# The high part of a normalised row written by ScalarE from x, its f32 row formed a second time by GpSimd

## The reference

```python
x = x + _L0_conv_ref(_gn(x), L0_conv_qkv_w, L0_conv_qkv_b, L0_conv_bias_table)
x = x + _L1_conv_ref(_gn(x), L1_conv_W, L1_conv_b)
...
qkv = (part @ qkv_w.T + qkv_b).reshape(n * NW, WS, 3, N_HEAD, HEAD_DIM)
...
attn = jnp.einsum('wihd,wjhd->whij', q, k)
attn = attn.reshape(n, NW, N_HEAD, WS, WS) + bias[None, None] + MASK[None, :, None]
attn = jax.nn.softmax(attn, axis=-1).reshape(n * NW, N_HEAD, WS, WS)
out = jnp.einsum('whij,wjhd->wihd', attn, v).reshape(n * NW, WS, c)
```

## Time and profile before

| | |
|---|---|
| median of 3 runs | 491.32 us (489.51 to 492.27) |
| the profiled execution | 492.15 us, of which its span is 490.3 us |
| busy share of the span | PE 84%, DVE 82%, ACT 78%, POOL 57% |
| granted TensorE clock, mean | 0.965 |

### The profile page before, as it was taken

The page is one execution under the profiler, slowest core; times in us unless marked ns, Lnnn a source line. Parts: engine busy times, 40 slices in busy tenths (PEclk is TensorE's granted clock), DMA queues, the critical chain, the costliest instruction groups (busy, mean ns, idle before and its releaser), DMA issues.

```text
span 490.3 us, 22208 instructions
## 1 busy us (share of the span) xinstructions
PE 411.5 (84%) x9320; PEld 346.6 (71%) x9320; DVE 400.0 (82%) x872; ACT 381.0 (78%) x913; POOL 280.1 (57%) x392
## 2 busy tenths in 40 slices
PE   0366846989899899988989998899899976799996
PEld 0365735877777778777777877777777765688885
DVE  6766856798789889987988898898787875699887
ACT  3377866898899899898889988899899866646550
POOL 5635746567767766675576677766766547430000
PEclk9987977999999999999999999999999988999999
DMA  6322220233323233323332323222222220033333
GB/s 207 115 86 67 83 95 1 89 98 91 99 91 99 87 102 95 102 78 105 94 105 93 97 94 99 92 76 75 73 73 71 73 69 5 21 130 129 141 138 130
DMA packets 42488, 44.98 MB, mean 92 GB/s; under 512 B 8082, under 2 KB 33940, under 8 KB 42388
## 3 DMA queue, kind: packets, MB, share of 16 engines
q1 hardware_dynamic: 41632, 43.55, 27.0%
q10 hardware_dynamic: 756, 0.01, 0.1%
HBM read 9.97 MB, written 8.39 MB: 37 GB/s over the span
## 4 chain that ended last, share of the span: by engine, by line
PE 40%; ACT 18%; SPq 12%; POOL 11%; issue 7%; DVE 6%; DMA 5%; ACTq 0%; POOLq 0%; DVEq 0%
SPq L315 11%; PE pv_ps L1053 5%; DMA k_stack<-k_flat 4%; PE proj_ps L938 4%; ACT k_flat L509 4%; POOL p_lo L442 4%; PE score_ps L1027 4%; PE proj_ps L940 3%; PE proj_ps L939 3%; PE proj_ps L927 3%; PE pv_ps L927 3%; PE score_ps L927 3%; ACT v_hi L526 3%; PE max_ps L927 3%; POOL xn_lo L395 2%
## 5 line engine op out<-in xcount | busy, mean ns | idle before, releaser
L442 POOL TENSOR_TENSOR p_lo<-probs,p_hi 128x512 f16<-128x512 f32 x128 | 146.6, 1166 | 111.1 <-ACT p_hi L608 77.9
L607 ACT ACTIVATE probs<-score_ps 128x512 f32<-128x512 f32 x128 | 76.9, 601 | 22.9 <-PE score_ps L1027 18.7
L788 DVE TENSOR_REDUCE neg_max<-max_ps 128x16 f16<-128x1024 f32 x64 | 78.4, 1224 | 15.8 <-PE max_ps L998 14.8
L938 PE MATMUL proj_ps<-xn_hi,w_hi 128*128 128x256 f32 x256 | 79.6, 311 | 12.5 <-POOL xn_lo L395 9.0
L608 ACT ACTIVATE p_hi<-score_ps 128x512 f16<-128x512 f32 x128 | 77.2, 603 | 0.0
L939 PE MATMUL proj_ps<-xn_lo,w_hi 128*128 128x256 f32 x256 | 74.2, 290 | 0.0
L940 PE MATMUL proj_ps<-xn_hi,w_lo 128*128 128x256 f32 x256 | 73.9, 289 | 0.0
L782 DVE TENSOR_TENSOR v_lo<-proj_ps,v_hi 64x256 f16<-64x256 f32 x128 | 54.2, 424 | 23.4 <-ACT v_hi L526 21.8
L938 PEld LDWEIGHTS proj_ps<-xn_hi,w_hi 128*128 128x128 f32 x256 | 51.2, 200 | 17.7 <-issue 13.3
L1027 PEld LDWEIGHTS score_ps<-max_rows,pick_max 64*64 64x64 f16 x1024 | 17.0, 107 | 62.9 <-ACT max_rows L598 62.3
L1053 PE MATMUL pv_ps<-v_hi,p_hi 128*128 128x68 f16 x512 | 57.0, 199 | 2.8 <-POOL p_lo L442 2.8
(11 more groups left out here) (129 smaller groups left out, 1150.7 us busy)
## 6 DMA issues: line engine op xcount, KB each, us to landing
q_stack<-q_flat SPq DMA_DIRECT2D x192, 64.0 KB
k_stack<-k_flat SPq DMA_DIRECT2D x192, 64.0 KB
xc<-in_x_dram SPq DMA_DIRECT2D x32, 256.0 KB, 3.5
out_dram<-xc SPq DMA_DIRECT2D x32, 256.0 KB, 2.4
w_raw<-in_qkv_w_dram SPq DMA_DIRECT2D x1, 768.0 KB, 6.8
bias_raw<-in_bias_table_dram SPq DMA_DIRECT2D x16, 32.0 KB
w_lif<-in_lif_w_dram SPq DMA_DIRECT2D x1, 256.0 KB, 4.7
b_cols<-in_qkv_b_dram ACTq DMA_DIRECT2D x4, 0.2 KB
```

What stands on the lines that cost most here:

```text
L442: pool.tensor_tensor(p_lo[p][:, quads, :, :].rearrange("p g w i -> p (g w i)"), probs[:, quads, :, :].rearrange("p g w i -> p (g w i)"), p ...
L607: act.activation(probs[:, quads, :, :].rearrange("p g w i -> p (g w i)"), score_ps[:, h, :], ACT.Exp)
L788: dve.tensor_reduce(neg_max[:, :].rearrange("p (m n) -> p m n", m=2)[:, :, 0:8], max_ps[:, :, :].rearrange("p m (n j) -> p m n j", j=WS), ...
L938: pe.matmul(dst, w_hi[:, c, cols], high[:, tok], start=(c == 0), stop=False)
```

## The change

Before, ACT makes `xn` from x (two instructions of 128 x 256 a row), then copies it to `xn_hi` (one of 128 x 512), and POOL subtracts. After, ACT writes `xn_hi` straight from x with the same two instructions, their output type fp32r, in p0 where the copy stood, and POOL forms `xn` from x for itself with two `tensor_scalar` instructions of 128 x 256 (times `rstd`, plus `shift`), at the end of p1, and waits for them before the next pair's `xn_lo`.

```diff
+            def normalise(slot, row, sample, norm, done):
+                pool.wait_ge(norm_ready, norm)
+                wait(pool, xn_lo_done, done - 1)
+                for h in range(HALVES):
+                    tok = slice(h * ROWTOK, (h + 1) * ROWTOK)
+                    col = bass.ds(sample * HALVES + h, 1)
+                    last = pool.tensor_scalar(xn[slot][:, tok], one(xc, row)[:, tok], rstd[:, col], shift[:, col], ALU.mult, ALU.add)
+                last.then_inc(xn_done, 1)
...
             def low_part(slot, done):
+                pool.wait_ge(xn_done, done)
                 pool.wait_ge(xn_hi_done, done)
+                wait(pool, v_ps_done, done - 2)
...
+            normalise(0, 0, 0, 1, 1)
             low_part(0, 1)
...
+                if p == 1 and not is_last_row(row, 3):
+                    ahead_sample = s + (k // 2 + 3) // WROWS
+                    normalise((k // 2 + 1) % 2, row + 3, ahead_sample, ahead_sample + 1, row + 4)
+                    pool.wait_ge(xn_done, row + 4)
...
-            def xn_high(slot, done):
-                act.wait_ge(xn_done, done)
+            def xn_high(row, sample, slot, norm, done):
                 wait(act, v_ps_done, done - 2)
-                act.activation(xn_hi[slot][:, :], xn[slot][:, :], ACT.Copy).then_inc(xn_hi_done, 1)
+                wait(act, xn_lo_done, done - 2)
+                normed(xn_hi[slot], row, sample, norm).then_inc(xn_hi_done, 1)
...
                 if p == 0 and not is_first(n, 1) and not is_last_row(row, 2):
-                    xn_high(k // 2 % 2, row + 3)
+                    ahead_sample = s + (k // 2 + 2) // WROWS
+                    xn_high(row + 2, ahead_sample, k // 2 % 2, ahead_sample + 1, row + 3)
                 if p == 1:
-                    sample = s + (k // 2 + 3) // WROWS
-                    for h in range(HALVES):
-                        if not is_last_row(row, 3):
-                            normalise(row + 3, sample, nxt % 2, sample + 1, row + 3, (h,))
-                        if not is_last_row(row, 2):
-                            (q_high, k_high)[h](row + 3)
+                    if not is_last_row(row, 2):
+                        q_high(row + 3)
+                        k_high(row + 3)
```

More of the change, by code:

```diff
@@ L408, in _ @@
             pool.wait_ge(const_step, 10)
+            normalise(1, 1, 0, 1, 2)
             low_part(1, 2)
+            normalise(0, 2, 0, 1, 3)
             pool.wait_ge(xn_lo_done, 2)
+            pool.wait_ge(xn_done, 3)
             def bias_low(v):
@@ L548, in _ @@
                 last.then_inc(setup_act, 1)
-            normalise(0, 0, 0, 1, 0)
-            xn_high(0, 1)
-            normalise(1, 0, 1, 1, 1)
+            xn_high(0, 0, 0, 1, 1)
             act.wait_ge(setup_dve, 3)
@@ L554, in _ @@
             q_high(1)
-            xn_high(1, 2)
+            xn_high(1, 0, 1, 1, 2)
             k_high(1)
@@ L559, in _ @@
             v_high(0, 1, 1)
-            normalise(2, 0, 0, 1, 2)
             bias_high(0)
@@ L610, in pair @@
                 if is_first(n, 1):
-                    xn_high(0, 3)
+                    xn_high(2, 0, 0, 1, 3)
                     bias_high(1)
```

## The result

Median of 4 executions after: 498.99 us (497.24 to 501.98), against 491.79 us for 4 before: a ratio of 1.0153, 95% interval 1.0082 to 1.0225. The change made the kernel 1.5% slower (7.2 us by the medians); the forecast was 496, about 1% slower (4.8 us). The profiled execution took 500.15 us with a span of 498.3, 8.0 more than the span of before.

The account below looks back on a forecast made before the run. ACT bounds B, PE bounds A. Six samples at +0.34 (+2.0), rows outside +0.9 and the start +1.9 make +4.8 us: 492.15 becomes 497.0, forecast 496 since the profiled execution lay 0.8 above the median; range 490 to 506.

Parts of the forecast that it names:

- the start: First rows: 2.0 us for a later first xn_lo, plus 0.9, less 1.0 in the sixth pair: +1.9 us.
- ACT's part: Two normalising instructions (0.99 us) replace a 0.52 us copy ahead of v_hi: B +0.47; removals in ordinary A worth 0.
- B: Half-row from p1's last scores on PE to the next p0's, bounded by ACT: 4.63 us undisturbed, forecast 5.10.
- A: Half-row from p0 to p1, read at max_rows, bounded by PE: 6.19 us, forecast 6.33.
- POOL's part: POOL's normalising at p1's end delays xn_lo, so project_q waits 0.14 us and all of A behind it.
- N: Time of POOL's two normalising instructions ahead of xn_lo, with the pass through xn_done: 1.1 us (ends 0.6 and 1.55).
- the excess of B: Mean B of 4.98 against undisturbed 4.63, put down to k_stack transfers: 0.35 us a half, taken as gone.
- nearly all of it under ACT's longer `xn_hi`: In the row with the roots, p_lo reaches PE 0.52 us late, nearly all hidden on ACT: that B is 5.15.
- cheap: Rival, N below 0.96: xn_lo is in time, A stays 6.19; about 491 us, no change; chance 0.25.
- dear: Rival, N = 1.55: project_q waits 0.59, a sample 47.5; about 509 us; chance 0.1 shared with the transfers rival.
- Faster: Rival: ACT paces A, -0.75 us a row for 29 rows; about 470 us, or 486 between; chance 0.1.
- the transfers keep their waits: Rival: k_stack waits add to B, 1.4 us a sample more; about 505 us; chance 0.1 shared with the dear rival.

Follow-up runs that it names:

- the fourth experiment: Kernel before, with ACT's copy to xn_hi replaced by the two instructions from x; ACT still forms xn in p1: median 498.39 us, ratio 1.0128.
- the third experiment: Kernel before, without the two ACT instructions that form xn in each pair, so later rows use old data: one execution, 489.28 us.
- the last experiment: Eighth of eight: changed kernel, with DVE's first bias addition held back until the first xn_lo is done: one execution, 498.73 us.
- the first experiment: Changed kernel, with POOL's two normalising instructions moved from the end of p1 to its start: median 494.97 us, ratio 1.0059.
- the fifth experiment: Kernel before, with POOL's two normalising instructions added at the end of p1, writing a spare tile nothing reads: one execution, 508.34 us.
- second: Changed kernel, with ACT also writing the first row's xn and POOL's first two instructions removed: median 495.94 us, ratio 1.0097.
- seventh: Changed kernel, POOL's normalising at p1's start, ACT writing the first xn, and xn_hi moved into p1 except behind the roots: median 489.9 us, ratio 0.9955.
- the sixth: Changed kernel, with POOL's normalising at the start of p1 and ACT writing the first row's xn: median 492.71 us, ratio 0.9996.

## Why the prediction was right, point by point

Sign and range were right, and the mechanism was the one forecast. The size came out too small: the sum was 4.8 us, the profiles differ by 8.0 and the medians by 7.2. Two terms were mis-sized: the six samples took 1.7 us more than forecast, the start 2.05 more. The rows outside, forecast at 0.9, brought 0.3.

**ACT's part: right.** 0.99 for the two instructions: 208.28 - 207.30 = 0.98. B was to be 5.10 and is 5.09; the fourth experiment gets this number by ACT's edit alone. A gains nothing from less work on ACT: the third experiment shows it, and so does ACT's idle time of 0.50 and 0.52 us ahead of `q_flat` and `k_flat` in the row shown.

**POOL's part: right in its direction, and in its sum by luck, since two errors cancel.** The instruction was forecast at 0.53 us and takes 0.557; N, from POOL's first to `xn_lo`'s start, is 210.29 - 209.06 = 1.23, not 1.1. The 0.21 us that the Trainium skill's page GPSIMD Engine Reference (4.1 Engine selection) led to as an estimate is refuted by the same row. How much of the 0.557 us grows with the size is not shown; POOL's steps of 128 x 2, of another form, already take 0.19 us (211.52). In the row shown `project_q` starts 211.61 - 209.43 = 2.18 us behind U, 0.35 later than the 1.83 of the earlier trace rows, where 0.14 was forecast. But "all of half A behind it" was wrong: A grew by 0.10 there and by 0.09 in the mean, since most of the lateness falls into slack that PE had further on. Before, PE paused between the q and the k projection, here in row 29 (PE, then its weight load, which waits for ACT's `attn_cm`):

```profile
389.14 0.28 PE L940 MATMUL proj_ps<-xn_hi,w_lo 128*128 128x256 f32 x1
389.40 0.38 PE L938 MATMUL proj_ps<-xn_hi,w_hi 128*128 128x256 f32 x1
389.63 0.28 PE L939 MATMUL proj_ps<-xn_lo,w_hi 128*128 128x256 f32 x1
```

```profile
389.40 0.19 PEld L938 LDWEIGHTS proj_ps<-xn_hi,w_hi 128*128 128x128 f32 x1 [0.18 <-ACT attn_cm L571]
```

and after it doesn't:

```profile
212.99 0.28 PE L947 MATMUL proj_ps<-xn_hi,w_lo 128*128 128x256 f32 x1
213.10 0.28 PE L945 MATMUL proj_ps<-xn_hi,w_hi 128*128 128x256 f32 x1
213.22 0.28 PE L946 MATMUL proj_ps<-xn_lo,w_hi 128*128 128x256 f32 x1
```

From start to start it was 0.26 and 0.23 us, and is 0.11 and 0.12, the pitch within a projection: 0.26 of the 0.35 is hidden there, and 0.10 is what A grew by. A later q projection finds `attn_cm` done when the k projection wants it (such waits of PE's weight loads: 18 before, 3.0 us; 4 after, 0.7 us). Four A halves came to 25.1, forecast 25.3: -0.2 a sample.

**Mis-sized: the excess of B, +0.5 a sample.** "I take the excess of 0.35 a half as gone": the waits for `k_stack` fell to 4.3 us, not to nothing. And "nearly all of it under ACT's longer `xn_hi`" is the step whose reasoning failed. The roots' `p_lo` ended at T + 12.87 (217.21 - 204.34; forecast 12.77). In the row shown PE did not wait for it: the transfers of `k_stack` had held PE up by 0.62 us already, and the weighing started at 217.35. In four of the six boundary halves PE did wait for `p_lo`, 0.17 to 0.57 us. In two of these, with waits of 0.41 and 0.42 us, the forecast's reasoning holds: B is 5.20, where 5.15 was forecast. But PE's lateness reaches ACT not through the v projection alone: `turn_attention` (L1070) comes before it, and its result is taken by `attn_cm`, which stands on ACT ahead of `xn_hi`. In the row shown ACT idled 0.29 us ahead of `attn_cm` (218.62), and the longer `xn_hi` then began late itself. A stall ahead of a longer instruction adds to it, and is not covered by it. Of the 24 B halves seven are longer than 5.25, 5.41 to 5.95, and these are the seven in which `attn_cm` waits for L1070; ahead of it PE waited for `k_stack` in four of them, for `p_lo` in one, for both in another; in the last only the weight load ahead of `max_scores` shows 0.30 us for `k_stack`. The boundary's six B halves have a mean of 5.32 (forecast 5.15), the other 18 of 5.21 (forecast 5.10): 0.17 + 3 x 0.11 = 0.5. With -0.2 in A that is the sample's 46.05 against the forecast 45.77, 1.7 us in six.

**Mis-sized: the start, forecast 1.9, profiled 3.95.** For the first `xn_lo` 2.0 was taken between 1.1 and 2.9; it was 2.66, near the end at which the addition slips in, and the last experiment shows that it is the addition. The Trainium skill's page SBUF — State Buffer (SBUF: two separate sides) calls the port pair that the two engines share an exclusive lock, held for a whole instruction; the trace agrees in so far as POOL's instruction of 18.89 ends behind the addition, by 0.39 us, after 2.15 us. At `max_rows` of the second pair the change is 53.66 - 49.03 = 4.63 late (0.7 of it comes back by the counted samples, where the forecast had 1.0 less 0.47): 2.66 from `xn_lo` and 1.97 behind it, of which the forecast had only 0.47. From PE's first projection to this `max_rows` the changed kernel took 22.53 to 53.66 = 31.13 us, the kernel before 19.87 to 49.03 = 29.16. But the first experiment's kernel, whose program is that of the change up to the first p1, took 29.30; and the fifth's, whose program is that of the kernel before up to the end of the first p1, took 31.00. These stretches by windows, before, after, first and fifth experiment (from, to, length, busy time of PE, PEld, DVE, ACT, POOL with counts, granted clock as a share of 2.4 GHz, DMA share, GB/s):

```profile
19.87:49.03 29.16, 21.08 (x274) 19.10 (x274) 17.84 (x37) 19.18 (x47) 10.99 (x20) 0.82 0.20 64
```

```profile
22.53:53.66 31.13, 22.96 (x274) 20.93 (x274) 16.17 (x36) 17.99 (x46) 13.34 (x24) 0.78 0.18 61
```

```profile
21.70:51.00 29.30, 20.22 (x274) 18.11 (x274) 16.30 (x36) 17.97 (x45) 14.47 (x26) 0.88 0.19 64
```

```profile
20.20:51.20 31.00, 23.29 (x274) 21.27 (x274) 17.82 (x37) 19.12 (x47) 10.97 (x20) 0.78 0.19 61
```

The same 274 matmuls ran at a mean clock of 0.82, 0.78, 0.88 and 0.78, each a mean over time at 2.4 and at 1.2 GHz. The stretch is short, 29.2 to 29.4 us, in the profiles of the kernel before and of the first, second, third and seventh experiments (clock 0.82 to 0.88), and long, 30.9 to 31.4, in those of the change and of the fourth, fifth, sixth and eighth (0.78 each). In the changed kernel PE was busy for 7.1 of the first ten us (clock 0.94), and the next ten were granted 0.72; in the first experiment it was busy for the same 7.1 (clock 1.00), and the next ten were granted 1.00, and the fall came after them (0.63). So some 2 us of the start go with the clock that an execution was granted. The changed start is neither needed for the low one (fifth experiment) nor does it bring it about each time (first experiment).

Whether the change makes it more frequent is open. The other executions say a little: those of the kernel before took 490.5 to 492.9 us at a mean granted clock of 0.965 and 493.5 to 494.9 at 0.962; the changed kernel took 497.24 and 497.82 at 0.966 and 500.15 at 0.962. At like clocks that is about 6 us more, so that some 1 us of the measured 7.2 may go with the clock that these four executions were granted. The fourth execution of the changed kernel, 501.98 at 0.959, fits less well (493.22 is the one before at 0.960).

**The rivals.** POOL's row is not cheap, since N is above 0.96, and not dear, since N is 1.23 and not 1.55. Faster is refuted by the third experiment. That the transfers keep their waits is true to about a third, 0.11 of 0.35 a half in ordinary rows.

## What to carry to other kernels

An engine that is idle 40% of the time may have none of it at the place where new work is put: read there what it does before and behind, and who waits for the next of its results; here the same two instructions one block earlier cost 0.9% less. Price an edit on a second engine in the half of the loop that this engine bounds: ACT lost 16 us of work where PE set the pace and gained 0.47 us a row where ACT did, and the kernel became slower. A stall is hidden under a longer instruction only if it arrives behind that instruction's start: follow it to the first instruction in the queue that it can hold.

## What the runs showed that I had not expected

- POOL's one-input `tensor_scalar` of 128 x 256 f32 takes 557 ns, and 2149 ns beside a two-input addition of DVE; with that addition put off, the pair and `xn_lo` ended 2.0 us earlier.
- The transfers of `k_stack` take and give back part of what an edit changes: their waits on PE's weight loads were 8.5 and 10.3 us where an undisturbed row, A and B, takes 10.8 us (before, third experiment), 3.6 to 6.2 us where it takes 11.3 to 11.4 (after; first, second, fourth, fifth and eighth experiments), and 8.9 us in the sixth, 2.6 of it in one wait. They go with the length of the row and not with that of B: in the fifth experiment a row takes 11.3 us with a B of 4.63, and the waits are 3.9 us. Gains and losses in B came out smaller than the single row says.
- The first 30 us of PE's work differ by 2 us between profiles, with the granted clock (0.78 against 0.82 to 0.88); that is over a quarter of the 7.2 us that the change cost.
- One wait of PE in the middle of the pairs can cost more than its length. Behind waits of 1.4 to 2.4 us the granted clock fell to 0.50, and the half that followed or held the wait grew by 1.3 to 3.6 us (third, fifth and sixth experiments, five such halves). It did not fall behind three waits of 2.1 to 2.4 us in the fifth experiment.
